# A decoder layer on one core: four program blocks joined into one, with every value tile ahead of the first self-attention scores

## What is computed

```python
h  = x + attn(x)                 # 32 heads of 16, causal, alibi bias, wqkv 512->1536, wout 512->512
h  = layernorm(h)                # "first" norm
h  = h + xattn(h, ctx, ctx, mask)# 32 query heads, 8 key/value groups, head width 128, rope on q and k
h  = layernorm(h)                # "second" norm
y  = relu(h@up)**2 @ down + (top-2 gate sum) * latent expert path
y  = layernorm(y)*gamma + beta
out = layernorm(h + y)
```

## Time and profile before

| | |
|---|---|
| median of 3 runs | 995.8 us (995.36 to 997.18) |
| the profiled execution, its own time | 994.21 us |
| its span, first to last instruction | 992.3 us |
| TensorE busy | 922.1 us, 93% |
| VectorE / ScalarE / GpSimd busy | 697.4 / 500.0 / 467.1 us |
| mean granted TensorE clock | 0.96 of full speed |

### The profile page before, as it was taken

The page is one execution under the profiler, slowest core; times in us unless marked ns, Lnnn a source line. Parts: engine busy times, 40 slices in busy tenths (PEclk is TensorE's granted clock), DMA queues, the critical chain, the costliest instruction groups (busy, mean ns, idle before and its releaser), DMA issues. The chain is left out here.

```text
span 992.3 us, 15681 instructions
## 1 busy us (share of the span) xinstructions
PE 922.1 (93%) x4812; PEld 776.6 (78%) x4812; DVE 697.4 (70%) x2195; ACT 500.0 (50%) x1565; POOL 467.1 (47%) x390
## 2 busy tenths in 40 slices
PE   7975999999998678999999999999999997799996
PEld 6754888888886557888888888888888885588885
DVE  5355688777777556777777777777777778674646
ACT  5233988777774225545545544554554555251220
POOL 4465543222222556666666566666666645321101
PEclk9977899999998978999999999999999999899998
DMA  7666577566662611112031211313112102200000
GB/s 265 231 250 130 149 196 183 133 129 149 138 182 86 243 32 33 33 52 108 33 125 35 100 51 43 118 33 127 33 32 107 35 20 85 95 13 22 22 7 37
DMA packets 68386, 96.63 MB, mean 97 GB/s; under 512 B 6096, under 2 KB 43216, under 8 KB 67152
## 3 DMA queue, kind: packets, MB, share of 16 engines
q1 hardware_dynamic: 68304, 95.64, 32.4%
HBM read 68.33 MB, written 27.26 MB: 96 GB/s over the span
## 5 line engine op out<-in xcount | busy, mean ns | idle before, releaser
L929 ACT ACTIVATE C_qh<-C_t 128x512 fp32r<-128x512 f32 x64 | 40.5, 633 | 181.3 <-POOL C_t L1128 181.3
L34 PE MATMUL C_pj<-xTh,wh 128*128 128x512 f32 x256 | 102.3, 399 | 6.2 <-DVE xTl L128 5.9
L34 PE MATMUL C_yb<-woh,C_oh 128*128 128x512 f32 x256 | 104.3, 408 | 3.1 <-DVE C_ol L1098 2.2
L1132 POOL TENSOR_TENSOR C_ql<-C_t,C_qh 128x512 fp32r<-128x512 f32 x64 | 82.7, 1292 | 47.6 <-ACT C_qh L929 47.6
L670 ACT ACTIVATE B_prob<-B_prob,B_top 128x128 f32<-128x128 f32 x256 | 99.0, 390 | 7.3 <-DVE B_top L774 7.3
L34 PE MATMUL C_pj<-xTl,wh 128*128 128x512 f32 x256 | 101.8, 398 | 0.0
L34 PE MATMUL C_pj<-xTh,wl 128*128 128x512 f32 x256 | 101.7, 397 | 0.0
L34 PE MATMUL C_yb<-woh,C_ol 128*128 128x512 f32 x256 | 101.6, 397 | 0.0
L34 PE MATMUL C_yb<-wol,C_oh 128*128 128x512 f32 x256 | 101.6, 397 | 0.0
L950 ACT ACTIVATE C_prob<-C_prob,C_top 128x128 f32<-128x128 f32 x256 | 99.0, 391 | 0.0
L1128 POOL TENSOR_TENSOR C_t<-C_t 128x512 f32<-128x512 f32 x64 | 83.0, 1297 | 18.4 <-DVE C_t L1058 18.4
(11 more groups left out here) (237 smaller groups left out, 2739.3 us busy)
## 6 DMA issues: line engine op xcount, KB each, us to landing
kv<-cross_kv_d SPq DMA_DIRECT2D x8, 2048.0 KB, 8.4
cross_kv_d<-B_k_out SPq DMA_DIRECT2D x16, 512.0 KB, 3.3
cross_kv_d<-B_v_out SPq DMA_DIRECT2D x16, 512.0 KB, 4.5
stage<-wq_dram SPq DMA_DIRECT2D x32, 256.0 KB, 2.7
stage<-wo_dram SPq DMA_DIRECT2D x32, 256.0 KB, 2.9
heads_q_d<-cTl SPq DMA_DIRECT2D x16, 256.0 KB
heads_k_d<-cTl SPq DMA_DIRECT2D x16, 256.0 KB
heads_q<-heads_q_d SPq DMA_DIRECT2D x32, 128.0 KB, 3.9
```

Of the source, the lines that this page charges most:

```text
L34: mm = eng.matmul(out, stationary[i], moving[j], start=first and n == 0, stop=last and n == len(PASSES) - 1)
L1132: eng.tensor_tensor(query(r, 1), by_batch(t1[:, r % 2, :]), query(r, 0).bitcast(F32), ALU.subtract).then_inc(s_qlo, 1)
```

## The change

The four functions become four classes (`ProjectSelf`, `AttendSelf`, `AttendCross`, `FeedForward`) whose methods emit the instructions of one step for one engine, and one block holds them all: an engine goes from the last tile of A to step 0 of B without meeting the others. All buffers have fixed addresses (`Chip`), and what used to be kept apart by the end of a block is now kept apart by waits on semaphores of the stage before. There is one ring of 5 slots for all weight pieces of B, C and D.

What it does part by part:

- **A.** The same 24 tiles, all of them ahead of step 0 of B (`BEFORE = QK + 8`, so `LATE = 0`: the code that could put value tiles into the steps of B does nothing here). The 2 MB load of x1 and the addition of `bout` leave A.
- **B.** x1 comes in eight loads of 256 KB, issued at steps 0 to 7, and `bout` is added at steps 6 to 13 on GpSimd. The projections' halves start at step 3 (`OFF = 3`), k tiles and v tiles alternate in pairs over both banks, `wk`'s piece is split at step 2 and those of `wv` at steps 3 to 6. The product with `wout` comes at G = 7, one step earlier. The first norm is made row by row: statistics, root, normalise, transpose, split at steps 8(b+2) to 8(b+2)+3. B gets 12 steps after its 64, in which the last halves, 8 weight pieces of C and four query projections lie.
- **C.** Step 0 starts with scores(0), and its minima come before the first rotation. Projections read `xT` in a new layout `[P, B, 2, C, S]`: the moving operand of one matmul is four runs of 128 columns, each from another batch, where it was one run of 512.
- **D.** Splits of 13 pieces at steps 58 to 64 of C, all low parts on GpSimd; the second norm row by row from step 59, transposes one a step from step 61, "lat" tiles at steps 60 and 61, the "up" tiles from step 65 on, among the last steps of C.

The core of the diff:

```diff
-        with ExitStack() as self_ctx:
-            ...
-            project_self(nc, xT0, wqkvT, bqk, bv, alibi_d, x_nat, bout, ident_d, ...)
-            attend_self(nc, ident[:, :], vhl, x1, heads, norms[0], cT, trig_sb, kv_d, ...)
-        attend_cross(nc, mask, trig_sb, ident[:, :], xT, w, kv, kv_d, wo_sb, x1, ...)
-        feed_forward(nc, down, gate, gamma, beta, power[:, :], xT, w, stage, x1, ...)
+        block = ctx.enter_context(nc.Block())
+        @block.tensor
+        def _(eng):
+            a.tensor(eng)
+            for n in range(b.STEPS):
+                b.tensor(eng, n)
+            for n in range(c.STEPS):
+                d.tensor_ahead(eng, n)
+                c.transpose(eng, n)
+                c.scores(eng, n)
+                c.outputs(eng, n)
+                d.tensor_between(eng, n)
+                c.values(eng, n)
+                c.queries(eng, n)
+                d.tensor_behind(eng, n)
+            d.tensor(eng)
 class ProjectSelf
-                if i == C:
-                    eng.dma_start(x1[:, :, :], x_d).then_inc(s_x, 16)
+    BEFORE = QK + 8
 class AttendSelf
-    OFF, TILES = 2, 2 * NG + 2 * B
+    LATE = B - (ProjectSelf.BEFORE - ProjectSelf.QK)
+    OFF = 3
+    FILL = [(kind, 2 * i + j) for i in range(NG) for kind in ("k", "v") for j in range(2)]
+    STEPS = NS + 12
+    PIECES = (("k", 0, 2), ("v", 0, 3), ("v", 1, 4), ("v", 2, 5), ("v", 3, 6), ("k", 1, 7), ("o", 0, 8), ...
+    NEXT_LOAD = {57: range(5), 62: (5, 6), 69: (7, 8), 71: (9,), 72: (10,)}
+    NEXT_SPLIT = {60: 0, 61: 1, 67: 2, 68: 3, 69: 4, 70: 5, 71: 6, 72: 7}
+    QUERY = {66: 0, 67: 1, 69: 2, 71: 3}
+    ROTATE = {67: 0, 68: 1, 70: 2, 72: 3}
+            if n < B:
+                eng.dma_start(self.x1[:, n, :], self.dram["x_nat"][:, n, :]).then_inc(self.s_x[n], 16)
+        b = self.normal(n, 0)
+        if b is not None:
+            eng.wait_ge(self.s_z, b + 1)
+            self.rows.statistics(eng, b)
+        b = self.normal(n, 1)
+        if b is not None:
+            self.rows.normalise(eng, b)
+        b = self.normal(n, 3)
+        if b is not None:
+            self.rows.lo(eng, b)
 class AttendCross
+            mm = product(eng, self.pj[r % 2], [t[:, c * P:(c + 1) * P] for t in self.w[j]],
+                         [self.rows.xT[:, 4 * half:4 * half + 4, lo, c, :] for lo in range(2)], c == 0, c == C - 1)
+        if n == 0:
+            self.minima(eng, n)
+        if n + self.PRE < self.TILES:
+            self.rotate(eng, n + self.PRE)
 class FeedForward
+    SPLIT = {58: (0, 1), 59: (2, 3), 60: (4, 5), 61: (6, 7), 62: (8, 9), 63: (10, 11), 64: (12,)}
+    STATS, NORMAL, TURN, TAKE = 59, 60, 61, 62
+    LAT = (60, 61)
+    FIRST = 65
```

More of the change, by code:

```diff
@@ new lines, in vector, with gpsimd_tile @@
+    def vector(self, eng):
+        for n in range(self.AHEAD):
+            self.piece_lo(eng, n)
+        for i in range(self.BEFORE):
+            self.vector_tile(eng, i)
+    def gpsimd_tile(self, eng, i):
+        kind, m, h = self.order[i]
+        eng.wait_ge(self.s_vhi, i + 1)
+        src = self.val[:, i % 2, :]
+        if kind == "qk":
+            hi, lo = (self.tiles[i % self.heads.RING][:, j, :] for j in range(2))
+        else:
+            src = src.rearrange("p (h d) -> p h d", d=DH)
+            hi, lo = self.vhl[:, m, :, 0:DH], self.vhl[:, m, :, DH:2 * DH]
+        eng.tensor_tensor(lo, src, hi.bitcast(F32), ALU.subtract).then_inc(self.s_vlo, 1)
@@ L508, in attend_self @@
+class AttendSelf:
     LT, LV = 2, 4
@@ new lines, in normal, with tile, splits, target @@
+    def normal(self, n, G):
+        b = n // NG - 2
+        return b if n % NG == G and 0 <= b < B else None
+    def tile(self, kind, n, lag):
+        f, odd = divmod(n - self.OFF - 2 - lag, 2)
+        return self.FILL[f][1] if not odd and 0 <= f < len(self.FILL) and self.FILL[f][0] == kind else None
+    def splits(self, n):
+        return [i for i, piece in enumerate(self.PIECES) if piece[2] == n]
+    def target(self, i):
+        kind, j, _ = self.PIECES[i]
+        return [t[:, :] for t in self.wk] if kind == "k" else [t[:, j % C, :] for t in (self.wv if kind == "v" else self.wout)]
@@ new lines, in project @@
+    def project(self, eng, f, part):
+        kind, i = self.FILL[f]
+        out = self.pj[i % 2]
+        if part == 0:
+            if f == 0:
+                eng.wait_ge(self.before.s_val, len(self.before.order))
+            if f >= 2:
+                freed, j = self.FILL[f - 2]
+                eng.wait_ge(self.s_sin if freed == "k" else self.s_vlo, j + 1)
+            eng.wait_ge(self.ring.s_lo, self.piece_at["k", i // 2] + 1 if kind == "k" else self.piece_at["v", i // B * C + C - 1] + 1)
+            if kind == "k" and i < 2:
+                eng.wait_ge(self.before.s_lo, self.before.CONTEXT + C * (i + 1))
+        for c in range(2 * part, 2 * part + 2):
+            if kind == "k":
+                st = [t[:, c * P:(c + 1) * P] for t in self.wk]
+                mv = [t[:, c, i % 2 * HALF:(i % 2 + 1) * HALF] for t in self.cT]
+            else:
+                st = [t[:, c, i % B * S:(i % B + 1) * S] for t in self.cT]
+                mv = [t[:, c, :] for t in self.wv]
+            mm = product(eng, out, st, mv, c == 0, c == C - 1)
+        if part == 1:
+            mm.then_inc(self.s_pj, 1)
@@ L614, in _ @@
-            loop(eng, step)
-            eng.wait_ge(s_kout, 16 * TILES // 2)
-            for i in range(2):
-                eng.wait_ge(s_vout[i], 16 * TILES // 4)
+            a.sync(eng, ring, b.sources())
+            b.sync(eng)
+            c.sync(eng)
+            d.sync(eng)
+        @block.scalar
+        def _(eng):
+            a.scalar(eng)
+            for n in range(b.STEPS):
+                b.scalar(eng, n)
+            for n in range(c.STEPS):
+                d.scalar_ahead(eng, n)
+                c.scalar(eng, n)
+                d.scalar_between(eng, n)
+            d.scalar(eng)
@@ L619, in _ @@
+        @block.vector
+        def _(eng):
+            a.vector(eng)
+            for n in range(b.STEPS):
+                b.vector(eng, n)
+            for n in range(c.STEPS):
+                d.vector_ahead(eng, n)
+                c.vector(eng, n)
+                d.vector_between(eng, n)
+            d.vector(eng)
         @block.gpsimd
         def _(eng):
[L621 to L635 removed]
@@ L1499, in tables @@
+            a.gpsimd(eng)
+            for n in range(b.STEPS):
+                b.gpsimd(eng, n)
+            for n in range(c.STEPS):
+                c.gpsimd(eng, n)
+                d.gpsimd_between(eng, n)
+            d.gpsimd(eng)
 def tables():
```

2286 lines of the change are left out of this document (1120 added, 1166 removed).

## The result

The changed kernel takes 1009.05 us (1005.79 to 1011.2, 4 runs), the kernel before beside it 995.58: a ratio of 1.0139, interval 1.0117 to 1.0161. It is slower by some 14 us, where 31 less were forecast. The profiled execution has a span of 1006.7 us.

A forecast was written before the change was run, and what follows sets the result against it. TensorE is never idle for 723 us and no matmul goes, so gains must come from the other four stretches. The terms -8 + 5.5 - 16 + 0 - 12 = -30.5 us gave 965 against the median; range 942 to 985.

The forecast's parts named there:

- The long stretch of B: B's steps: none cheaper; transposes 2.6 us, waits 2 for eight batches, later heads' loads 1; together +5.5 us.
- Rival 2: B becomes bound by VectorE and ScalarE; losing 2.3 us a batch makes it 16 us more, 981; chance 0.19.
- The transposes: Six of the eight rows' transposes move into B's long stretch, 0.44 us each: 2.6 us.
- The seam from C to D: Step 60 of C to the first gate product of D: 71 us against 83.2, gain 12, bounds 5 and 18.
- The front: A and B's first steps: first half projection at 92.3 us instead of 100.08; gain 8, bounds 2 and 14.
- The heads' loads behind x1: In B, batch 1's heads queue behind four rows of x1 on SyncE: 0 to 3.4 us, 1 taken.
- The seam from B to C: B's last scores to step 3 of C: 65 us against 81.3, gain 16, bounds 8 and 28.
- The long stretch of C: C's steps: same instructions in the same order, except four runs of 128 columns as moving operand; 0 us.
- the tail: End of the kernel, the chain of the last row's norms: unchanged, 9.3 us.
- rival 3: Matmuls of C and D reading four runs of 128 columns cost more; 30 ns each eats the gain; chance 0.05.
- Rival 4: Waits replacing the blocks' ends cost what these did; time stays within 2 us of 996; chance 0.04.

The follow-up runs named there:

- e_all2: Changed kernel with the moves of `e_bout`, `e_order`, `e_seamd`, `e_seamc`, `e_wk`, beta added row by row, lat tiles' parts at step start: 961.92 us, ratio 0.9682.
- e_bout: Changed kernel with GpSimd's eight additions of bout spread over B's steps, in a buffer of their own: 1002.32 us, ratio 1.0078.
- e_order: Changed kernel with VectorE's row statistics behind the key tile's rotation and ScalarE's row copy ahead of the exponentials in B: 986.4 us, ratio 0.9921.
- e_seamd: Changed kernel with, from C to D, GpSimd's root at the next step's start and VectorE's normalisation at that step's end: 999.57 us, ratio 1.0054.
- e_wk: Changed kernel with wk's first piece split at step 0 of B instead of step 2: 1002.42 us, ratio 1.0107.
- e_late4: Changed kernel with the last four value tiles made in steps 0 to 3 of B instead of ahead of step 0: 1015.17 us, ratio 1.0213.
- e_stats: Changed kernel with only VectorE's row statistics moved behind the rotation of the key tile in B: 993.87 us, ratio 0.9996.
- e_copy: Changed kernel with only ScalarE's copy of the row's transposes moved ahead of the four exponentials in B: 999.43 us, ratio 1.0047.
- e_seamc: Changed kernel with high and low parts of the four query tiles one step behind their rotations, from B to C: 1005.79 us, ratio 1.0095.

## Why the prediction was wrong

Faster was forecast, and 1009 lies beyond the range of 942 to 985. The work was counted nearly right: in `e_all2` every line of the ledger is within 3.5 us of its forecast. What failed are two terms for waits, and one stall was not thought of.

**The long stretch of B: this step failed.** "About 2 us of wait against a slack of two steps of 2.9 us. I take 2 us for the eight batches" became 14.3 us in the changed kernel's own trace (172.5 less 158.2) and 17.5 in `e_bout`'s (175.7): some 7.1 for the wait for the copy, 4.0 for the statistics, and 3.2 for each 6.8 us at half clock. The slack of two steps is not there, because VectorE works in order: behind its wait at G = 3 stands the low part of the next step's probabilities, and TensorE needs that one step on. The other wait, statistics ahead of the rotation at G = 0, was not named at all: 0.68 + 0.18 + 0.15 us of work were counted as VectorE's share, not as something that a bank of TensorE stands behind. Rival 2 named the wait at G = 3 and nearly the price (16 us), but that the price fits is in part luck: the statistics were not in it, nor the half clock, and its heading, B bound by VectorE and ScalarE, is not what happened, since `e_order` takes no work from either. With 0.19 it got too small a chance, and it was worked out as if the other terms held. The transposes (2.6 us) fit the remainder of 4.9.

**The seam from C to D: this step failed too.** "VectorE about 6.1 us a step against TensorE's 5.2 for four steps, 4 us; I give 4 more for GpSimd" counted work per engine. What set the time was order: 10.4 us were VectorE standing for a root behind two low parts (`e_seamd`), 5.5 the second lat tile standing for the low part of the first (`e_all2`), half clock behind these waits counted in. With both orders mended the seam takes 68.7 us against the 71.2 forecast, so the counted work was nearly right.

**The front: right in its mechanism, too large.** Tile 9 was at 41.61 (forecast 40.6), tile 12 at 50.01 (49.0), the last tile at 86.9 (83.9): ScalarE waited three times more for DMAs (1.2, 0.5 and 1.6 us, the stores and a piece of the context), where the forecast had no wait at all. The first exponential came at 87.8 (85.1), the first half projection at 94.9 (92.3), 5.2 us earlier than before. Step 8 gained 4.3 instead of 7, and the 2.7 us that it lacks are there already at the first exponential. The low part of wk stood in TensorE's queue ahead of the scores (`e_wk`). The clock was half from 83.5 to 104.0 us, behind TensorE's waits; before it was from 87.7 to 104.7. The Trainium skill, "TensorE: Matmul & The Clock Gate" ("HAM oscillation — how this bites in real kernels"), says that such waits put the clock back, and the prediction's estimate by it was 5 of the 8. The six matmuls of the first projection in 2.90 us agree with the rule; the gains of 4.3 and 5.2 near its 5 are partly luck, as ScalarE's waits came on top. Taken for every wait the rule doesn't hold: from 150 to 300 us TensorE stood ten times for 1.1 us and the granted clock was 1.00; it fell at 301.9, behind the eleventh.

**The heads' loads behind x1: right.** 1 us was taken, none was lost to the loads. Step 8 started 4.4 us after step 7, 1.5 more than a plain step, and what TensorE waited for was GpSimd's low part of wv. Of the 3.4 us that the prediction made due by "DMA: Bandwidth & Descriptors" ("Queues, rings and completion order") of the Trainium skill nothing shows, and this is no test of it: the four rows of x1 had landed at 93.8 us, the heads' loads were issued from 95.2 on and had landed at 102.4, 11 us ahead of step 8.

**The seam from B to C: right, too large by 5.** 70.1 against 65.3, within the bounds. Scores(0) of C came 44.2 us after scores(63) instead of 39; step 3 came 25.9 us later, for which 23 and 3 of half clock had been allowed. GpSimd's fourteen operations and the root took the 24 us counted (342.4 to 366.6, scores(0) at 366.7), but they began 19.9 us after scores(63), not 15.

**The long stretch of C and the tail.** 427.8 against 427.0: rival 3 is out, a matmul that reads four runs of 128 columns starts 0.227 us after the one before, as the others. Rival 4 is out as stated, since the seam from B to C did close by 11 us; that the total comes near it is the sum of a gain and larger losses. From the gate on 2.0 us were lost in this execution, 0.4 in that of `e_bout` with the same code there (8.5 and 4.5 us at half clock).

**Not foreseen: the hold at step 14.** 4.75 us and half clock behind it in the profiled execution. It took 5.16 us in `e_late4` and 1.48 to 1.50 in the profiled executions of `e_order`, `e_stats`, `e_copy`, `e_seamd`, `e_seamc` and `e_wk`, all with the same additions. So its share in the 14 us differs from execution to execution.

The ledger closes: -4.3 + 25.6 - 11.2 + 0.8 + 1.4 + 2.0 = +14.3 against 14.4 us of span.

**What stays open.** What decides between a hold of 1.5 and one of 5.2 us for the same code: only profiled executions show it, so how often the long one comes, and how much of the 14 us of the medians it is, is not known. And why the half clock in the seam from B to C lasts 17 us in one execution and 27 to 31 in another, by which its 69 to 76 us for one code differ.

## What to carry to other kernels

Where TensorE is full and the other engines are at 75 to 80%, an operation added to a step costs by what stands behind it in its queue, not by its length: 1 us of statistics and a 0.6 us copy cost 14 to 17 us over six batches at one place in the step, and at another they fit, with all else that the change added there, into 5. So before adding work to a tight loop, go through each engine's order and ask of each new wait who is queued behind it and which bank or buffer that one frees; a root of 0.55 us that everyone needs goes ahead of low parts that nobody waits for yet. And joining stages pays only once this is done: the same joined program is 1.4% slower or 3.2% faster than the four blocks, with the same operations.

## What the runs showed of the hardware

- The scaling, an operation of VectorE over two operands in SBUF, waits for an operation of GpSimd in progress: it takes 0.42 us alone and 0.81 to 0.83 where it meets a low part near the middle, and operations that read a bank keep their 0.28 and 0.69 us beside 10.2 us of additions. The Trainium skill, "SBUF — State Buffer" ("Who interferes with whom"), says that a VectorE instruction with two SBUF inputs contends with a GpSimd one that reads SBUF, and, of VectorE's two-port modes, that whoever issues first has the shared ports for the whole instruction while the other blocks. The 0.81 and 1.5 us agree; 5.17 us go over four operations of GpSimd, which that rule does not give, and 0.42 in the midst of eight shows that one can also get in between.

```profile
126.77 1.27 POOL L166 TENSOR_TENSOR B_wout<-stage,B_wout 128x512 fp32r<-128x512 f32 x1
126.83 1.50 DVE L813 TENSOR_TENSOR B_o<-B_o,B_rden 128x256 f32<-128x256 f32 x1
128.01 3.95 POOL L610 TENSOR_TENSOR x<-x,B_bout 128x512 f32<-128x512 f32 x3
```

These lines are of `e_seamd`, in order of time. Again VectorE began 0.06 us behind GpSimd; here it came in after one operation, and the three additions took 3.95 us, 0.23 more than the 3.72 of the long hold.

- Half clock costs TensorE time in a stretch that it fills: in B's long stretch 6.8 us at a granted clock of 0.50 added some 3.2 us, step 58 took 6.05 us there, and 3.36 at the same place of the four batches before it, at full clock.
